# Sixteen instead of twenty-four projection groups, and eight heads of probabilities in flight, in a fused attention and expert layer

## The chip, the cores and the metric

One core of a Trainium2 chip runs the whole kernel in one launch. The core has TensorE (PE, matrix products), VectorE (DVE), ScalarE (ACT), GpSimd (POOL) and SyncE (SP, here used only to issue DMAs), each with its own instruction stream; they meet only at semaphores. SBUF is the memory of 128 partitions that all of them share, PSUM the eight banks that PE writes to. The metric is the device time of one execution in microseconds; lower is better.

## What is computed

One transformer layer on x of shape [32, 256, 128], all in float32:

```
xn = layernorm(x)
Q, K, V = xn @ W_qkv            # 16 heads of 64, per sample of 256 tokens
Q, K[first 32 of 64] = q * cos + rotate_half(q) * sin
scores = where(causal, -inf, Q K^T) / sqrt(64);  attn = softmax(scores) V
out = x + attn @ W_o + moe(xn)
moe: softmax over 9 logits, the top 2 chosen; 8 experts of 128 -> 512 (gelu) -> 128,
     the ninth choice passes xn through; each weighted with its gate
```

`rotate_half` takes the halves (x1, x2) of a head's 32 rotary values to (-x2, x1).

## The kernel before

**Stages.** A prologue loads and normalises all 64 tiles of tokens and transposes them (`xnT_hi`, `xnT_lo`: each float32 is split in two float16 numbers, and a product of two such pairs is three float16 matmuls, `split3`). Then the projections of sample 0 are made, the router decides (DVE), and the attention loop runs over 32 samples. Last come the experts over 104 tiles of sorted tokens and the gathering of their results.

**A sample** is 16 steps, one head each. On every engine a step `s` of sample `b` does the work of several heads, each a fixed number of steps behind:

- PE: scores of head s (4 matmuls, `scores`), then the projection units that `BESIDE[s]` lists (for the next sample, or the output product `y` of the last one), then the three transposes of head s-3's probabilities (`T_LAG`), and in every second step the product with V for two heads (`attend`, `PV_LAG` 5).
- DVE: `invert` (reciprocal of head s-2's sums), `mask` (causal mask and row maximum), an eviction of transposes for every fourth head, the work on a unit's result one step later (`turn`, `rest_low`, `y_add`), low parts of k's rotated rows (`k_rope_low`), low part of the attention output (`o_low`); in step 0 `dispatch` (normalises two tiles of tokens to `send_x` after waiting that the four sends of the sample before have landed) and `mix`.
- ACT: `rest_high`, `o_high`, transposes' evictions, `rope_high`, and the two exponentials of head s (`exps`).
- POOL: `scale` of head s-2 (two instructions, L432 and L433), `q_rope_low` (L422), `rope_add` (L417), and in steps 1, 9, 12 and 14 (`SEND_AT`) one indirect DMA (`send`, L437) that scatters 128 token rows to DRAM. Before each of the last three sends, and so before the scale of that step, POOL waits for the send before it (L448).
- SP: `stack_q(b + 1)` once q's rotated low parts are done, then `stack_k(b + 1)`.

**Projection units.** Q and K weights lie in 24 groups of 128 rows: 8 of rotary rows (four heads x 32 rows each), 8 of the other rows, and 8 more with the rotary rows in swapped order, so that `rotate_half` comes out of the matmul. A `rope` unit (8 a sample) makes one group and its swapped twin side by side in a PSUM bank; DVE multiplies the 512 columns with a table of cos and sin (`turned`, two buffers), POOL adds the two halves to `roped` (four buffers), ACT rounds to float16, POOL (q) or DVE (k) makes the low part. A `rest` unit (4 a sample) makes two groups without rotation. Three PSUM banks (`PJ`) go round among the units; two hold scores, two transposes, one the products with V.

**Stacking.** The scores product contracts over 128 partitions: 64 values of a head twice. SP's DMAs gather them inside SBUF: for each r of 4, two DMAs of 64 rows x 4 KB for q and two of 64 rows x 2 KB for k, 16 DMAs and 3 MB a sample. PE waits in steps 0, 4, 8 and 12 for group r = s/4 of both. The stacks have two buffers, the staging tiles (`q_staged`, `k_staged`) one.

The order on each engine is the order written in the code; nothing is reordered by a planner.

## Time and profile before

| | |
|---|---|
| median of 3 runs | 1582.79 us (1578.91 to 1585.89) |
| span of the profiled execution | 1643.9 us |
| looped samples 1 to 30 | 146.72 to 1190.99 us of the span |
| busy share PE, ACT, DVE, POOL | 82%, 71%, 70%, 60% |
| DMA share in the loop | about 0.44 |

The span goes from the first to the last instruction of one execution under the profiler; that execution has no other time, and it is 61 us longer than the median of the others. The first `L1108` of a sample is its first scores matmul: the tile it reads changes between `second` and `arena` from sample to sample, which is how a sample's start is found. A line number is a line of the kernel before.

### The profile page before, as it was taken

To read this page: it belongs to the slowest core of one execution; us is meant where nothing else is said; L and a number is where in the kernel's file an instruction comes from. 1 tells how busy PE (TensorE), PEld (TensorE's weight loads), DVE (VectorE), ACT (ScalarE), POOL (GpSimd) and SP (SyncE) were. 2 spreads that over 40 slices of the span, in tenths; PEclk is the share of its full clock that TensorE was granted. 3 is DMA by queue.
4 is the path that set the end of the run, shared out by engine and by line. 5 is a ranking of instruction groups with operands and counts; after the bars stand their busy time and mean duration, and the time that the engine had idled before them with its cause. 6 is when DMAs were issued, how large, how long until landed. Compare 5 with 4: busy or idle time off the path is not lost.

```text
span 1643.9 us, 48543 instructions
## 1 busy us (share of the span) xinstructions
PE 1341.7 (82%) x13156; PEld 1038.9 (63%) x13157; DVE 1143.8 (70%) x4325; ACT 1174.3 (71%) x3758; POOL 987.4 (60%) x1697
## 2 busy tenths in 40 slices
PE   2529999999999999999999999999977999576620
PEld 1417766777666776766777667766656988455520
DVE  6788776777777777767777777777756777354531
ACT  7409887888888888878888878888877888334310
POOL 3208777777777787777777777776760000454555
PEclk9859999999999999999999999999998999788865
DMA  9623544334553335543345433355423333222242
GB/s 302 164 49 83 115 115 102 86 84 97 115 119 87 86 84 109 120 104 86 85 93 117 117 91 85 84 110 117 105 89 94 87 85 85 72 77 77 79 129 64
DMA packets 125894, 166.49 MB, mean 101 GB/s; under 512 B 15504, under 2 KB 85392, under 8 KB 125456
## 3 DMA queue, kind: packets, MB, share of 16 engines
q1 hardware_dynamic: 117296, 147.50, 37.6%
q0 software_dynamic: 8416, 17.33, 3.6%
q14 instruction: 161, 1.32, 0.3%
q8 instruction: 21, 0.34, 0.1%
HBM read 30.42 MB, written 33.69 MB: 39 GB/s over the span
## 4 chain that ended last, share of the span: by engine, by line
POOL 30%; issue 20%; PE 18%; DMA 16%; DVE 7%; another core or an unknown queue 3%; ACT 2%; DVEq 1%; POOLq 1%; SPq 1%; ACTq 0%
DMA sorted_x_dram<-send_x,send_at 15%; POOL probs L433 8%; POOL probs L432 7%; POOL arena L417 7%; PE bank L1034 4%; PE bank L1033 4%; PE bank L1035 4%; POOL arena L422 4%; POOL sorted_x_dram L437 3%; PE bank L1132 1%; PE bank L1166 1%; PE bank L1118 1%; DVE arena L690 1%; POOL arena L482 1%
## 5 line engine op out<-in xcount | busy, mean ns | idle before, releaser
L577 ACT ACTIVATE probs<-arena,neg_max 128x128 f32<-128x128 f32 (+1 forms) x1024 | 455.4, 448 | 126.5 <-DVE neg_max L887 112.1
L432 POOL TENSOR_TENSOR probs<-probs,inv_total 128x128 f32<-128x128 f32 x512 | 208.2, 407 | 247.8 <-DMA sorted_x_dram<-send_x,send_at 126.4
L1118 PE MATMUL bank<-ident,probs 128*128 128x128 f32 x1536 | 263.2, 280 | 70.6 <-POOL probs L433 62.6
L887 DVE CUSTOM_DVE_ANT_0 arena<-bank,causal 128x128 f32<-128x128 f32 (+1 forms) x1024 | 314.9, 345 | 0.0
L482 POOL DMA_INDIRECT arena<-sorted_y_dram,slots x128 | 123.7, 967 | 273.6 <-DMA sorted_y_dram<-arena 171.6
L1118 PEld LDWEIGHTS bank<-ident,probs 128*128 128x128 f32 x1536 | 173.6, 141 | 144.9 <-issue 87.9
L894 DVE RECIPROCAL inv_total<-total 128x2 f32<-128x2 f32 x512 | 82.9, 162 | 254.4 <-PE bank L1109 178.1
L433 POOL TENSOR_SCALAR probs<-probs,inv_total 128x256 f32<-128x256 f32 x512 | 251.4, 491 | 0.0
L417 POOL TENSOR_TENSOR arena<-arena 128x256 f32<-128x256 f32 x256 | 189.8, 752 | 64.0 <-DVE arena L849 58.8
L1033 PE MATMUL bank<-xnT_lo,wqk_hi 128*128 (+1 forms) x768 | 212.2, 276 | 10.7 <-DVE arena L855 10.2
L1035 PE MATMUL bank<-xnT_hi,wqk_hi 128*128 (+1 forms) x768 | 212.1, 276 | 0.0
L1034 PE MATMUL bank<-xnT_hi,wqk_lo 128*128 (+1 forms) x768 | 211.9, 276 | 0.0
L577 ACT ACTIVATION_READ_ACCUMULATOR probs<-arena,neg_max 128x1 f32 x1024 | 195.3, 191 | 0.0
L558 ACT ACTIVATE probsT<-bank 128x384 f32<-128x384 f32 x384 | 186.0, 484 | 9.4 <-issue 9.0
L1132 PE MATMUL bank<-probsT,second 128*64 128x256 f32 x1024 | 169.2, 406 | 1.0 <-DVE arena L905 1.0
L849 DVE TENSOR_TENSOR arena<-bank,arena 128x512 f32<-128x512 f32 x256 | 169.2, 681 | 1.1 <-PE bank L1035 0.9
L437 POOL DMA_INDIRECT sorted_x_dram<-send_x,send_at x128 | 140.0, 1094 | 29.0 <-issue 21.0
L533 ACT ACTIVATE arena<-arena 128x256 f16<-128x256 f32 x256 | 106.7, 417 | 59.8 <-POOL arena L417 53.1
L1033 PE MATMUL bank<-second,arena 128*128 x640 | 123.4, 225 | 12.4 <-issue 8.5
L1034 PE MATMUL bank<-second,arena 128*128 x640 | 122.4, 225 | 13.4 <-issue 13.4
L636 ACT ACTIVATE arena<-bank 128x512 f32<-128x512 f32 x160 | 92.9, 598 | 55.4 <-remote 30.9
L1035 PE MATMUL bank<-second,arena 128*128 x640 | 121.8, 224 | 11.8 <-issue 11.6
(158 smaller groups left out, 3675.6 us busy)
## 6 DMA issues: line engine op xcount, KB each, us to landing
second<-arena SPq DMA_DIRECT2D x128, 256.0 KB, 4.2
arena<-arena SPq DMA_DIRECT2D x128, 256.0 KB, 4.1
second<-arena SPq DMA_DIRECT2D x128, 128.0 KB
arena<-arena SPq DMA_DIRECT2D x128, 128.0 KB
arena<-sorted_x_dram SPq DMA_DIRECT2D x80, 128.0 KB
sorted_y_dram<-arena SPq DMA_DIRECT2D x80, 128.0 KB
sorted_x_dram<-arena SPq DMA_DIRECT2D x3, 2560.0 KB, 21.2
arena<-experts_dram SPq DMA_DIRECT2D x8, 512.0 KB, 4.5
```

What stands on the lines that cost most here:

```text
L417: nc.gpsimd.tensor_tensor(roped[j % 4], t[:, 0:SEQ], t[:, SEQ:2 * SEQ], ALU.add).then_inc(rope_sum, 1)
L432: nc.gpsimd.tensor_tensor(p0, p0, inv_total[:, s % 4, 0:1].broadcast_to([P, P]), ALU.mult)
L433: nc.gpsimd.tensor_scalar(p1, p1, inv_total[:, s % 4, 1:2], 1.0, ALU.mult, ALU.mult).then_inc(p_ready, 1)
L437: nc.gpsimd.indirect_dma_start(out=sorted_x, out_offset=bass.IndirectOffsetOnAxis(ap=send_at[:, i:i + 1], axis=0), in_=send_x[:, i // TOP, ...
L558: nc.scalar.activation(probsT[:, s % 4, :], TP[s % 2][:, 0:PW], ACT.Copy).then_inc(t_out[1], 1)
L577: last = nc.scalar.activation(probs[:, s % 4, at:at + w], masked[:, s % 2, at:at + w], ACT.Exp, bias=neg_max[:, s % 2, t:t + 1], scale=-1. ...
L887: last = nc.vector.tensor_tensor_reduce(out=masked[:, s % 2, at:at + w], in0=SC[s % 2][:, at:at + w], in1=causal[:, at:at + w], scale=1.0, ...
L1033: mm(dst, a_hi, b_lo, start=start, stop=False)
L1034: mm(dst, a_lo, b_hi, start=False, stop=False)
L1035: return mm(dst, a_hi, b_hi, start=False, stop=stop)
L1118: last = nc.tensor.transpose(TP[s % 2][:, k * P:(k + 1) * P], probs[:, s % 4, k * P:(k + 1) * P], ident[:])
L1132: mm(PV[rows, :], v_sb[:, 0, vs], probsT[:, s % 4, 0:SEQ], start=True, stop=False)
```

## The change

The swapped copies of the rotary rows go away (24 groups become 16). The rotary rows are regrouped instead: a group now holds the first 16 rotary rows of eight heads, its partner the last 16 of the same heads. A `rope` unit makes such a pair, [x1 | x2] in one bank; DVE multiplies both by cos and both by sin (two instructions of 512 columns), POOL makes x1 cos - x2 sin and x2 cos + x1 sin (two instructions of 256). There are 4 rope units a sample instead of 8, one unit a step, and low and high parts are made on 512 columns at once. `by_cos` and `by_sin` have one buffer, `roped` two. The staging tiles hold rotary halves in another row order, so each r takes five DMAs instead of two for q and five for k (one of 64 rows, four of 32 rows whose sources are 16 rows): 40 a sample.

The freed PSUM bank (PJ goes from 3 to 2) gives a second bank for the products with V. The buffers of probabilities and their sums go from 4 to 8 heads; transposes run 4 steps behind instead of 3, evictions 5 instead of 4, products with V 7 instead of 5, the output 8 instead of 6. The identity tile and `half` move into the arena. The weights' high and low parts are made in 16 instructions each instead of one.

```diff
-PROLOGUE = ([("rest", 0), ("rest", 1)] + [("rope", j) for j in range(4)]
-            + [("rest", 2), ("rest", 3)] + [("rope", j) for j in range(4, 8)] + [("v_low", 0), ("v_low", 1)])
+PROLOGUE = [("rest", 0), ("rest", 1), ("rope", 0), ("rope", 1), ("rest", 2), ("rest", 3), ("rope", 2), ("rope", 3),
+            ("v_low", 0), ("v_low", 1)]
 BESIDE = [
-    [("rest", 0)], [("rest", 1), ("rope", 0)], [("rope", 1)], [("rope", 2), ("rope", 3)],
-    [("rest", 2)], [("rest", 3), ("rope", 4)], [], [("rope", 5), ("rope", 6)],
-    [("rope", 7)], [("v_high", 0), ("v_high", 1)], [], [("y", 0)],
-    [("v_low", 0)], [("y", 1)], [("v_low", 1)], [],
+    [("rest", 0)], [("rope", 0)], [("rest", 1)], [("rope", 1)],
+    [("rest", 2)], [("rope", 2)], [("rest", 3)], [("rope", 3)],
+    [("v_high", 0)], [], [("v_high", 1)], [("y", 0)],
+    [("y", 1)], [("v_low", 0)], [("v_low", 1)], [],
 ]
 SEND_AT = [1, 9, 12, 14]
-PJ_BANKS = 3
+PJ_BANKS = 2
+ROPES = 4
+POS = (0, 2, 1, 3)
+STACKED = 16 * 5
-INV_LAG, T_LAG, OUT_LAG, PV_LAG, O_LAG = 2, 3, 4, 5, 6
+INV_LAG, T_LAG, OUT_LAG, PV_LAG, O_LAG = 2, 4, 5, 7, 8
+HELD = 8
...
-        PJ, SC, TP = bank[0:3], bank[3:5], bank[5:7]
-        PV = bank[7][:, 0:SEQ]
+        PJ, SC, TP = bank[0:2], bank[2:4], bank[4:6]
+        PV = [b[:, 0:SEQ] for b in bank[6:8]]
...
-                sp.wait_ge(q_rope_lo, 4 * n + 4)
+                sp.wait_ge(q_rope_lo, 2 * n + 2)
                 for r in range(GRP):
-                    for half_at in range(2):
-                        sp.dma_start(q_stack[parity][64 * half_at:64 * half_at + 64, r, :, :].rearrange("p l n -> p (l n)"),
-                                     q_staged[32 * r:32 * r + 32, :, :, :].rearrange("p k l n -> p (k l n)")).then_inc(q_stacked[r], 16)
+                    sp.dma_start(q_stack[parity][64:128, r, :, :, :].rearrange("p h l n -> p (h l n)"),
+                                 q_rest[32 * r:32 * r + 32, :, :, :].rearrange("p h l n -> p (h l n)").unsqueeze(1)
+                                 .broadcast_to([32, 2, 2048])).then_inc(q_stacked[r], 16)
+                    for h in range(2):
+                        for c in range(2):
+                            rows = slice(64 * h + 16 * r, 64 * h + 16 * r + 16)
+                            sp.dma_start(q_stack[parity][32 * c:32 * c + 32, r, h, :, :].rearrange("p l n -> p (l n)"),
+                                         q_rope[rows, c, :, :].rearrange("p l n -> p (l n)").unsqueeze(1)
+                                         .broadcast_to([16, 2, 1024])).then_inc(q_stacked[r], 16)
...
-                sp.wait_ge(k_rope_lo, 4 * n + 4)
+                sp.wait_ge(k_rope_lo, 2 * n + 2)
                 for r in range(GRP):
-                    for half_at in range(2):
-                        sp.dma_start(k_stack[parity][64 * half_at:64 * half_at + 64, NG * r:NG * r + NG, :].rearrange("p h t -> p (h t)"),
-                                     k_staged[32 * r:32 * r + 32, half_at, :, :]).then_inc(k_stacked[r], 16)
+                    sp.dma_start(k_stack[parity][64:128, r, :, :].rearrange("p h n -> p (h n)"),
+                                 k_rest[32 * r:32 * r + 32, :, :, :].rearrange("p l h n -> p l (h n)")).then_inc(k_stacked[r], 16)
+                    for h in range(2):
+                        for c in range(2):
+                            rows = slice(64 * h + 16 * r, 64 * h + 16 * r + 16)
+                            sp.dma_start(k_stack[parity][32 * c:32 * c + 32, r, h, :],
+                                         k_rope[rows, c, :, :]).then_inc(k_stacked[r], 16)
...
-                nc.gpsimd.tensor_tensor(roped[j % 4], t[:, 0:SEQ], t[:, SEQ:2 * SEQ], ALU.add).then_inc(rope_sum, 1)
+                r = roped[j % 2]
+                nc.gpsimd.tensor_tensor(r[:, 0, :], by_cos[:, 0, :], by_sin[:, 1, :], ALU.subtract)
+                nc.gpsimd.tensor_tensor(r[:, 1, :], by_cos[:, 1, :], by_sin[:, 0, :], ALU.add).then_inc(rope_sum, 1)
...
-                    raw(wqk_hi[:].rearrange("p g n -> p (g n)"), raw_qk)
+                    for at, of in WQK:
+                        last = nc.scalar.activation(wqk_hi[:, at, :], of, ACT.Copy, scale=W_SCALE)
+                    last.then_inc(raw_hi, 1)
...
                 dve.wait_ge(pj_ready, u + 1)
-                if not (isinstance(m, int) and m == 0 and j < 2):
-                    dve.wait_ge(rope_sum, 8 * m + j - 1)
-                nc.vector.tensor_tensor(turned[j % 2], psum[:], rot_q if j < NG else rot_k,
-                                        ALU.mult).then_inc(turn_done, 1)
+                if not (isinstance(m, int) and m == 0 and j == 0):
+                    dve.wait_ge(rope_sum, ROPES * m + j)
+                nc.vector.tensor_tensor(by_cos, both, cos, ALU.mult)
+                nc.vector.tensor_tensor(by_sin, both, sin, ALU.mult).then_inc(turn_done, 1)
```

## Rows read from the trace of the kernel before

**Rows 1.** The page: span, and busy time, share and instructions of each engine.

```profile
span 1643.9 us, 48543 instructions
...
PE 1341.7 (82%) x13156; PEld 1038.9 (63%) x13157; DVE 1143.8 (70%) x4325; ACT 1174.3 (71%) x3758; POOL 987.4 (60%) x1697
```

**Rows 2.** Busy time by stretch, one sample in the middle; last columns clock, DMA, GB/s.

```profile
146.72:180.60 33.88, 32.10 (x309) 24.55 (x310) 26.42 (x118) 29.68 (x103) 25.62 (x48) 1.00 0.51 114
...
390.23:425.13 34.90, 32.45 (x311) 24.43 (x309) 26.48 (x116) 29.31 (x103) 26.66 (x49) 1.00 0.44 99
425.13:1190.99 765.86, 714.02 (x6776) 537.34 (x6777) 578.22 (x2528) 638.26 (x2199) 579.17 (x1057) 1.00 0.44 99
```

**Rows 3.** Waits in that sample: engine, line, releaser; us, times, longest.

```profile
POOL probs L432 <- DMA sorted_x_dram<-send_x,send_at: 4.3, 2, 2.9
...
PE bank L1118 <- POOL probs L433: 1.7, 4, 0.6
...
POOL arena L417 <- DVE arena L849: 1.4, 2, 0.7
...
PE bank L1118 <- ACT probsT L558: 0.5, 1, 0.5
```

**Rows 4.** Timeline of POOL in that sample.

```profile
397.73 0.73 POOL L417 TENSOR_TENSOR arena<-arena 128x256 f32<-128x256 f32 x1 [0.69 <-DVE arena L849]
...
413.08 1.18 POOL L437 DMA_INDIRECT sorted_x_dram<-send_x,send_at  x1 [0.16 <-issue]
...
419.07 0.40 POOL L432 TENSOR_TENSOR probs<-probs,inv_total 128x128 f32<-128x128 f32 x1 [2.94 <-DMA sorted_x_dram<-send_x,send_at]
...
423.43 0.40 POOL L432 TENSOR_TENSOR probs<-probs,inv_total 128x128 f32<-128x128 f32 x1 [1.41 <-DMA sorted_x_dram<-send_x,send_at]
```

**Rows 5.** Groups in that sample: busy us, mean ns; idle before, releaser.

```profile
L432 POOL TENSOR_TENSOR probs<-probs,inv_total 128x128 f32<-128x128 f32 x16 | 6.5, 404 | 6.0 <-DMA sorted_x_dram<-send_x,send_at 4.3 <-DVE inv_total L894 1.4
...
L417 POOL TENSOR_TENSOR arena<-arena 128x256 f32<-128x256 f32 x8 | 5.9, 753 | 1.6 <-DVE arena L849 1.4
...
L437 POOL DMA_INDIRECT sorted_x_dram<-send_x,send_at x5 | 5.4, 1080 | 0.8 <-issue 0.8
L849 DVE TENSOR_TENSOR arena<-bank,arena 128x512 f32<-128x512 f32 x8 | 5.3, 682 | 0.0
...
L422 POOL TENSOR_TENSOR arena<-arena 128x256 f16<-128x256 f32 x4 | 2.7, 682 | 0.0
```

**Rows 6.** Timeline of PE at the start of that sample: start, duration.

```profile
390.56 0.27 PE L1033 MATMUL bank<-xnT_lo,wqk_hi 128*128 x1
...
391.10 0.27 PE L1035 MATMUL bank<-xnT_hi,wqk_hi 128*128 x1
391.95 0.32 PE L1118 MATMUL bank<-ident,probs 128*128 128x128 f32 x1 [0.58 <-POOL probs L433]
```

**Rows 7.** Timeline of DVE in that sample, step 0.

```profile
392.49 0.60 DVE L828 TENSOR_SCALAR send_x<-acc,neg_mean,rstd 128x128 f32 x2 [0.46 <-DMA sorted_x_dram<-send_x,send_at]
```

**Rows 8.** Timeline of SP's DMA issues in that sample.

```profile
406.79 8.03 SPq L311 DMA_DIRECT2D arena<-arena  x8
415.82 6.45 SPq L318 DMA_DIRECT2D arena<-arena  x8
```

**Rows 9.** Chain that ended last, before the first looped sample.

```profile
132.20 0.54 SPq L311
...
142.10 4.39 DMA arena<-arena
...
146.72 0.23 PE bank L1108
```

**Rows 10.** Issues of three DMA lines: ns min/median/max, first and last start.

```profile
L311 SPq DMA_DIRECT2D arena<-arena x128: 537/1057/2015, 132.2 to 1180.5; - x128
...
L318 SPq DMA_DIRECT2D arena<-arena x128: 597/603/1697, 141.3 to 1188.2; - x128
...
L302 SPq DMA_DIRECT2D arena<-experts_dram x8: 327/429/435, 1191.4 to 1234.7; - x8
```

More of the change, by code:

```diff
@@ L255, in beside, with rest_parts, rope_parts @@
                     for n, (at, kind, j) in enumerate(units_of(first, last)) if at == s]
-        def parts(which, rest, g, n=1):
-            at = slice(g * SEQ, (g + n) * SEQ)
-            if which == 0:
-                return q_staged[:, rest, 0, at], q_staged[:, rest, 1, at]
-            return k_staged[:, 0, rest, at], k_staged[:, 1, rest, at]
+        def rest_parts(j):
+            return [q_rest[:, j % 2, n, :] if j < 2 else k_rest[:, n, j % 2, :] for n in range(2)]
+        def rope_parts(j):
+            of, at = q_rope if j < 2 else k_rope, slice(j % 2 * SEQ, (j % 2 + 1) * SEQ)
+            return [of[:, :, n, at] for n in range(2)]
         def owner(kind, b):
@@ L451, in sample @@
                     for kind, j, u, psum, n in beside(b, first, last, s - 3):
-                        if kind == "rope" and j < NG:
+                        if kind == "rope" and j < 2:
                             q_rope_low(j, b + 1)
@@ L700, in _ @@
                     low(rw_lo[:], rw_f[:], rw_hi[:], 1).then_inc(split, 1)
-                    low(wqk_lo[:].rearrange("p g n -> p (g n)"), raw_qk,
-                        wqk_hi[:].rearrange("p g n -> p (g n)"), 2).then_inc(split, 1)
+                    for at, of in WQK:
+                        hi, lo = wqk_hi[:, at, :], wqk_lo[:, at, :]
+                        if at < 8:
+                            hi, lo = (v.rearrange("p (r n) -> p r n", n=16) for v in (hi, lo))
+                        last = low(lo, of, hi, 2)
+                    last.then_inc(split, 1)
             low(wvo_lo[:].rearrange("p k n -> p (k n)"), raw_vo, wvo_hi[:].rearrange("p k n -> p (k n)"), 3).then_inc(split, 1)
@@ L1124, in attend @@
                     pe.wait_ge(v_ready, 4 * b + (2 if j == 0 else 4))
-                if not (first and j < 1):
-                    pe.wait_ge(o_done, 8 * b + j)
+                if not (first and j < 2):
+                    pe.wait_ge(o_done, 8 * b + j - 1)
                 for i in range(2):
@@ L1141, in sample @@
                     if not (first and s < T_LAG):
-                        transposes(G - T_LAG, (s - T_LAG) % 4, None if first and s < T_LAG + 2 else
+                        transposes(G - T_LAG, (s - T_LAG) % HELD, None if first and s < T_LAG + 2 else
                                    evicted(b, s - T_LAG - 2) if s >= T_LAG + 2 else evicted(b - 1, s - T_LAG - 2 + H))
```

153 lines of the change are left out of this document (82 added, 71 removed).

## The prediction

> **What bounds the kernel now.** I read the page first [rows 1]: no engine is full over the span (PE 82%, ACT 71%, DVE 70%, POOL 60%), so I cut it at the sample starts. The 30 looped samples run from 146.72 to 1190.99, 1044.3 us or 34.81 us each, at full TensorE clock [rows 2]. That stretch is 64% of the span and the change works almost only there; what lies before (147 us, mostly router and normalising) and behind (453 us, the last sample and the experts) keeps its work.
>
> Inside one typical sample (390.23 to 425.13) PE is busy 32.45 of 34.90 us, ACT 29.3, DVE 26.5, POOL 26.7 [rows 2]. PE looks like the limit, but its list of waits names POOL: before the transposes it waits 1.7 us for L433 and 0.5 for an ACT eviction that is itself one step behind [rows 3]. POOL in turn stands 4.3 us, twice, on the landing of an indirect send: the send issued at 413.08 is waited for until 419.07, 2.9 us of it with nothing else to do [rows 3, 4]. So POOL with 26.7 busy + 4.3 landing waits + 0.8 before the sends [rows 5] = 31.8 us is a chain that PE hangs on with a lag of only three heads; the other 3.1 us of its sample are waits for DVE (1.4 + 1.4, [rows 3, 5]) and crumbs. It is a two-way coupling: a late POOL delays PE, a late PE then starves POOL at the start of the next sample.
>
> **The change, part by part.**
>
> *Four projection units fewer on PE.* A rope unit is six matmuls; the six at 390.56 to 391.10 start 0.11 us apart [rows 6], so a unit is 6 x 0.109 = 0.655 us and four are 2.6 us a sample. PE's own need falls from at most 32.45 to at most 29.8 us (busy time counts overlapping tails, so the true need is lower). ACT's need stays under the 29.3 it has now.
>
> *The same rotation elsewhere.* DVE multiplied 8 x 512 elements (0.68 us each, [rows 5]); it now makes two 512-element multiplications for each of four units: 8 again. POOL added 8 x 256 (0.75 us) and still does. The four low parts of 256 (0.68 us) become two of 512, on POOL and on DVE: between half of now (only fixed cost) and all of it; I take the same. So DVE 26.5 and POOL 26.7 us are not relieved. The two products have one buffer now instead of two, so a turn waits for POOL's add of the unit before; units are two steps apart, which covers it (an add pair is 1.5 us against about 4 us of steps).
>
> *The longer pipeline (transposes four heads behind instead of three, values seven instead of five, eight probability buffers, two PV banks).* It hides POOL's landing stalls from PE: 1.7 + 0.5 us and the shadow they throw. It does not remove them from POOL: sends stay at steps 1, 9, 12 and 14. POOL's 31.8 us therefore remain as a cycle: add of unit 0, the scales, sends 1 to 3, landing of send 3, dispatch on DVE at step 0 (L828 already waits for it, [rows 7]), turn of unit 0, add of unit 0. The bound is 31.8 if sends land as now, and 29.3 if both landing waits shrink to what the slower steps cover (31.8 - 2.5: I leave 1.8 of 4.3). PSUM for projections goes from three banks to two, with one unit a step; the bank is read in the step after, so this costs nothing while DVE is less than a step late, and makes PE follow DVE's local pace when it is.
>
> *The stacking DMAs.* Now 8 for q and 8 for k a sample; afterwards 20 and 20 for the same 3 MB. Here I see the new danger. Today SP issues q over 8.03 us from 406.79, then k over 6.45 us from 415.82 [rows 8]. The first heads of the next sample need only k's group 0, but that is queued behind all of q. At the first looped boundary this chain already decides: q's first issue at 132.20, k's group 0 landed, PE starts at 146.72 [rows 9]: 14.5 us from rotation done to start. In the loop it has room: 406.79 + 14.5 = 421.3 against 425.13, 3.8 us.
>
> After the change the chain has 25 issues instead of 10. What does one cost? No row shows a copy of 32 rows inside SBUF. Floor: 0.33 us, the shortest issue of L302; ceiling: 0.64 us, the unblocked 0.60 of a 64-row k copy (L318) and 0.04 between issues [rows 8, 10]. Above L318's floor, q's median of 1.06 us is the 256 KB waiting for the queue. The form is nearest to L318's (three-dimensional source, SBUF on both sides), but half the rows; I take 0.58 spacing. Then q is 4 x 1.0 + 16 x 0.58 = 13.3 us at most, 11.6 if the large ones no longer queue; I take 12.3; k's first five 2.9 us; last landing about 1.6 us more: 16.8 us. Both ends: the bytes alone, as now, 14.0 less what overlaps, say 13.2 (spacing 0.37); 4 x 1.1 + 16 x 0.64 + 5 x 0.64 + 2.3 = 20.1.
>
> Where does it start? Now rotation of q is done 16.6 us after the sample's start (406.79 - 390.23) [rows 8]. The work up to there is the same on POOL (five scales, four adds of 256, low parts), but the first add can start earlier: it stands at 7.5 us (397.73, [rows 4]), of which about 1 us is PE's stall of 0.58 before the first transposes and its echo [rows 6]. So 15.5 us, minus little. The next sample can start at 15.5 + 16.8 = 32.3 us; ends 28.7 and 35.6.
>
> *A rule against the change.* A 64-row k copy of 128 KB goes out every 0.64 us, 205 GB/s, its source 32 partitions wide [rows 8, 10]. If the 16-partition sources drained at half that rate, the rope half of q (1 MB) would take 10.2 us instead of 5.1, q in all 15.3, and k's group 0 1.9 more with about 1 us landing: 18.2, so a sample of 33.7. The Trainium skill, page SBUF — State Buffer, section on the DMA port swizzle, says just this: a range of 16 partitions reaches 4 ports and one of 32 reaches 8, 104 against 189 GB/s at 1 MiB; its figure for the wide case fits the 205 seen here, and no run here shows the narrow one. By the page the estimate would be near that same 33.7 a sample.
>
> *Weights and prologue.* 16 weight groups instead of 24 but split by 16 instructions on ACT and DVE: before, 3,072 columns in one; now 2,048 in sixteen. About even. Ten units instead of fourteen before the router, where DVE's own work decides: nothing, give or take 2 us. The first boundary, already set by stacking, gets 16.8 - 14.5 = 2.3 us longer. Two more lags to drain at the end: +1 us, against a shorter stall.
>
> **The sum.** Two cycles lie almost on each other: POOL with its sends 31.8, stacking 32.3. I take 32.1 us a sample: 30 x (34.81 - 32.1) = 81 saved, less 2.3 and 1 = about 78 us of the profiled 1643.9 (there is no other time for that execution; it is 61 us above the median 1582.8, so it carries profiling cost). Taken off the median: 1505 us.
>
> **The rivals.**
> - *A, both cycles near 32 (31.2 to 33.2 a sample)*: 1477 to 1538. For it: two independent sums meet. 0.45.
> - *B, stacking stays hidden and the sends land earlier*, because small copies spread the traffic; the bound is then PE's 29.8 or POOL's 29.3, samples of 29.3 to 31.2: 30 x 3.6 to 5.5 less the 3.3 at the edges, so 1421 to 1477. For it: the 0.33 us issue. Against: DVE's dispatch still waits for send 3. 0.25.
> - *C, narrow sources at half rate*, or 0.64 and a queue: 33.2 to 34.5 a sample, 1538 to 1577. 0.15.
> - *D, no change*: the stall only moves from before the transposes to the sample's first scores, 34.5 to 35.0, 1577 to 1592. 0.05.
> - *E, slower*: SP's queue decides. With the start at 15.5 us the point is 34.8 - 15.5 = 19.3 us for 25 issues and a 1.6 us landing: 0.71 us a copy. At 0.80 us it is 21.6 us, a sample of 37.1, 30 x 2.3 = 69 us more and the 3: 1655. Against: no unblocked issue in the trace is over 0.6. 0.10.
>
> Range: out of it stay D and E (0.15) and the lowest fifth of B (0.05): 1432 to 1578. A's own range is 1477 to 1538. Faster by over 0.5% (8 us, about what a measurement of this kernel tells from no change): A, B, C = 0.85; within: 0.05; slower: 0.10.
>
> **What would show it.** Right: sample starts 32 us apart; PE's waits before L1118 for POOL gone in the loop; a wait of one to three us before the first L1108 of a sample, released by a stacking DMA; POOL still waiting some 3 to 4 us a sample for sends; PE busy about 30 of 32; L311's successor issued in about 12 us. Wrong: no DMA in front of L1108 (then B); spacing of narrow copies over 0.7 us (E); packets of 2 KB from 16 partitions lasting twice those of now (C); PE waiting for its projection banks on DVE, which I cost at nothing: if that shows, DVE's first nine steps of a sample are the limit, and a sample is longer by what it waits there. The step I trust least is the cost of a copy with 32 rows.

## The result

The changed kernel is slower: 1649.26 us (median of 4, 1642.40 to 1653.47) against 1580.85 us of the kernel before, a ratio of 1.041 [1.037, 1.045]. The forecast was 1505 us, its range 1432 to 1578. The outcome is that of rival E (1655 us, chance 0.10), and a part of the reason is E's.

From the page after, the span, the engines' busy time and SP's DMA queue:

```profile
span 1640.7 us, 46858 instructions
...
PE 1285.1 (78%) x12388; PEld 977.4 (60%) x12389; DVE 1115.2 (68%) x4276; ACT 1143.0 (70%) x3645; POOL 981.5 (60%) x1635
...
q1 hardware_dynamic: 145968, 147.03, 40.8%
```

Two spans can't be compared here. That of [rows 1] is 1643.9 and this one 1640.7, though the medians lie 68 us apart: behind the last head's scores (1221.3 before, 1278.6 after, from the trace) the execution of before took 422.6 us and this one 362.1. That is the expert stage, which both kernels share; it is told of at the end. So I compare samples, by the start of the first scores matmul of each.

Busy time by stretch: the 30 looped samples, then two samples in a row, then the step 0 of each of the two.

```profile
155.93:1251.98 1096.05, 939.39 (x8520) 683.86 (x8521) 761.47 (x3390) 835.05 (x2880) 783.13 (x1380) 0.95 0.46 95
376.58:413.04 36.46, 31.37 (x284) 22.84 (x285) 25.40 (x113) 27.75 (x97) 26.10 (x46) 0.95 0.46 95
413.04:448.00 34.96, 29.80 (x284) 21.94 (x285) 25.40 (x113) 27.73 (x97) 26.10 (x46) 1.00 0.48 99
376.58:380.27 3.69, 3.69 (x21) 2.40 (x22) 2.01 (x10) 1.34 (x6) 0.85 (x2) 0.57 0.45 101
413.04:415.26 2.22, 2.21 (x21) 1.68 (x21) 1.59 (x9) 0.85 (x4) 0.86 (x2) 1.00 0.35 83
```

A looped sample takes 1096.05 / 30 = 36.54 us, against 34.81 [rows 2]: 52 us of the 68. PE did lose its four units (29.80 us busy at full clock, against 32.45 [rows 2]; the forecast was at most 29.8), and every engine is less busy than before. What has grown is waiting, and PE's largest wait is in one place. Waits of the loop:

```profile
POOL probs L461 <- DVE inv_total L932: 229.3, 131, 6.3
...
PE bank L1145 <- DMA arena<-arena: 44.7, 15, 4.9
...
PE bank L1145 <- DMA second<-arena: 40.5, 15, 3.7
...
PE bank L1072 <- DVE arena L895: 34.2, 72, 1.5
...
POOL probs L461 <- DMA sorted_x_dram<-send_x,send_at: 26.0, 38, 2.4
```

L1145 is the scores matmul (L1108 before): in each of the 30 samples PE waits for a stacking DMA before its first head, 85.2 us in all, 2.8 us each. POOL's 4.3 us a sample for its sends [rows 3] have shrunk to 26.0 / 30 = 0.9, and POOL now waits 7.6 us a sample for DVE, which waits for PE: POOL is no longer a limit. L1072 <- L895 is the two-bank wait that I priced at nothing: 1.1 us a sample.

SP's issues of the first of those samples, and then the end of the chain to the next sample's start:

```profile
393.25 0.56 SPq L323 DMA_DIRECT2D second<-arena  x1
393.86 2.90 SPq L329 DMA_DIRECT2D second<-arena  x4
396.81 0.59 SPq L323 DMA_DIRECT2D second<-arena  x1
397.44 3.21 SPq L329 DMA_DIRECT2D second<-arena  x4
400.70 0.60 SPq L323 DMA_DIRECT2D second<-arena  x1
401.34 2.96 SPq L329 DMA_DIRECT2D second<-arena  x4
404.35 0.59 SPq L323 DMA_DIRECT2D second<-arena  x1
404.99 3.10 SPq L329 DMA_DIRECT2D second<-arena  x4
408.13 0.59 SPq L336 DMA_DIRECT2D second<-arena  x1
408.76 2.51 SPq L341 DMA_DIRECT2D second<-arena  x4
```

```profile
392.10 1.13 POOL arena L449
...
394.50 0.99 SPq L329
...
398.08 1.30 SPq L329
...
410.68 2.13 DMA second<-arena
412.82 0.23 issue
413.05 0.23 PE bank L1145
```

The first issue comes 16.7 us after the sample's start, q's 20 copies take 14.9 us, k's first five 3.1, and 1.8 later PE starts: 19.8 us of chain, and 36.5 in all. It replaces q's and k's rows of [rows 8]. The issue times, by line (L329 and L341 are the new 32-row copies, 16 source rows; ns min/median/max):

```profile
L329 SPq DMA_DIRECT2D second<-arena x256: 591/597/1845, 75.1 to 1209.6; - x128
```

```profile
L341 SPq DMA_DIRECT2D arena<-arena x256: 591/596/783, 151.8 to 1259.5; - x128
```

A copy of 32 rows costs SP what one of 64 rows did [rows 10]: 0.60 us, and 0.04 to the next. In each of the four q groups one 32-row copy takes longer, 1.0 to 1.3 us (two stand in the chain above).

There is a second loss that I hadn't thought of. After PE's wait its clock is at half: the 21 matmuls of step 0 take 3.69 us at a granted clock of 0.57 in the one sample and 2.22 us at 1.00 in the other. The other engines' step 0 follows, and q's first issue with it: 16.7 us after the start there, 15.1 us here (428.15 - 413.04).

All 30 samples fit this: from q's first issue to the next sample's start it is 19.5 to 20.3 us in each but the first two (20.9 and 21.3), and the samples differ by when that issue comes, 15.1 us after the start in the five even ones at full clock, 16.1 in the one odd sample at full clock, and 16.4 to 17.4 in the 24 whose step 0 ran below it. So each of them is the time to q's first issue plus a chain that hardly varies. The mean clock of the loop is 0.95 where it was 1.00 [rows 2], so about 110 us of it ran at 1.2 GHz. The Trainium skill, page TensorE: Matmul & The Clock Gate, section HAM oscillation, describes this pattern, a burst of matmuls, a wait for a DMA, and the next burst at half clock; the trace agrees in 24 of 30 samples, with 2.8 us of wait a sample on average and 1.5 us more for step 0 in the sample shown. The length of the wait alone doesn't tell the 24 from the other six: those waited 2.4 to 2.6 us, and one of the 24 waited 2.3.

### The profile page after: what moved, and what is told of

Its sections match the earlier page's. It is cut to its first block, busy times and chain, and to the rows that moved or that the text cites. A ratio compares the mean times of both kernels' runs of the same rounds, so it can differ in the third digit from the quotient of the medians.

```text
span 1640.7 us, 46858 instructions
## 1 busy us (share of the span) xinstructions
PE 1285.1 (78%) x12388; PEld 977.4 (60%) x12389; DVE 1115.2 (68%) x4276; ACT 1143.0 (70%) x3645; POOL 981.5 (60%) x1635
## 3 DMA queue, kind: packets, MB, share of 16 engines
q1 hardware_dynamic: 145968, 147.03, 40.8%
## 4 chain that ended last, share of the span: by engine, by line
PE 25%; SPq 24%; POOL 19%; issue 12%; DVE 10%; DMA 7%; ACT 2%; DVEq 1%; POOLq 0%; ACTq 0%
SPq L329 17%; PE bank L1072 5%; PE bank L1073 5%; PE bank L1074 4%; POOL arena L511 4%; SPq L323 4%; POOL probs L462 3%; PE bank L1170 3%; POOL probs L461 3%; POOL arena L449 3%; SPq L341 3%; PE bank L1156 2%; POOL arena L444 2%; DMA arena<-sorted_y_dram,slots 2%; DMA second<-arena 2%
## 5 line engine op out<-in xcount | busy, mean ns | idle before, releaser
L1156 PE MATMUL bank<-arena,probs 128*128 128x128 f32 x1536 | 265.2, 283 | 33.7 <-ACT probsT L589 26.6
L1156 PEld LDWEIGHTS bank<-arena,probs 128*128 128x128 f32 x1536 | 188.5, 146 | 82.9 <-ACT probsT L589 31.1
L1072 PE MATMUL bank<-xnT_lo,wqk_hi 128*128 (+1 forms) x512 | 150.8, 294 | 41.5 <-DVE arena L895 35.0
L943 DVE TENSOR_TENSOR arena<-bank,arena 128x256 f16<-128x256 f32 x256 | 106.6, 416 | 88.2 <-ACT arena L594 88.2
L466 POOL DMA_INDIRECT sorted_x_dram<-send_x,send_at x128 | 145.5, 1136 | 29.6 <-issue 20.3
L1074 PE MATMUL bank<-xnT_hi,wqk_hi 128*128 (+1 forms) x512 | 149.4, 292 | 0.0
L1145 PE MATMUL bank<-second 128*128 128x128 f16 (+1 forms) x512 | 103.8, 256 | 52.3 <-DMA second<-arena 40.5
L443 POOL TENSOR_TENSOR arena<-arena 128x256 f32<-128x256 f32 x128 | 105.5, 824 | 61.7 <-DVE arena L890 61.7
L1145 PE MATMUL bank<-arena 128*128 128x128 f16 (+1 forms) x512 | 104.0, 257 | 47.1 <-DMA arena<-arena 44.7
L564 ACT ACTIVATE arena<-arena 128x512 f16<-128x512 f32 x128 | 80.7, 630 | 71.8 <-POOL arena L444 71.7
L1072 PE MATMUL bank<-second,arena 128*128 x640 | 118.5, 222 | 3.1 <-DVE arena L1020 2.9
L1020 DVE TENSOR_TENSOR arena<-arena 128x512 f16<-128x512 f32 x160 | 109.4, 693 | 14.5 <-ACT arena L674 11.5
```

The costliest lines, as they stand in the source:

```text
L1072: mm(dst, a_hi, b_lo, start=start, stop=False)
L1074: return mm(dst, a_hi, b_hi, start=False, stop=stop)
L1145: mm(dst, q_lo, ks, start=True, stop=False)
L1156: last = nc.tensor.transpose(TP[s % 2][:, k * P:(k + 1) * P], probs[:, at, k * P:(k + 1) * P], ident[:])
```

## The experiments

Where only a ratio tells, it is against the kernel before in the same batch; its median there was 1584 us for e1, e3, e5 and e6, 1655 for e9 to e12, 1583 for e13 to e15, 1656 for e16 and 1653 for e17 to e19. Periods are means of the 30 looped samples, "odd" those that begin a turn of the loop (two samples a turn, so samples 1, 3, ...).

| run | ratio | interval | us a sample | odd / even |
|---|---|---|---|---|
| before | 1 | | 34.81 | 34.7 / 34.9 |
| after | 1.041 | 1.037 to 1.045 | 36.54 | 36.7 / 36.4 |
| e1 half the bytes | 1.038 | 1.035 to 1.040 | 36.76 | 36.8 / 36.7 |
| e6 before, 40 copies | 1.040 | 1.037 to 1.042 | 36.85 | 37.1 / 36.6 |
| e5 after, old lags | 1.030 | 1.027 to 1.033 | 36.30 | 36.2 / 36.5 |
| e3 k's group 0 earlier | 1.019 | 1.016 to 1.022 | 35.81 | 38.1 / 33.6 |
| e9 unrotated rows first | 1.004 | 1.003 to 1.006 | 35.20 | 37.1 / 33.3 |
| e10 the same, 32 copies | 1.002 | 1.001 to 1.003 | 34.90 | 36.6 / 33.2 |
| e11 as e9, old lags | 1.001 | 1.000 to 1.003 | 34.96 | 37.3 / 32.6 |
| e12 before, two banks | 1.148 | 1.145 to 1.150 | 42.77 | 42.9 / 42.7 |
| e13 as e10, 6 samples a turn | 0.978 | 0.976 to 0.979 | 33.55 | |
| e14 before, 6 a turn | 1.010 | 1.008 to 1.012 | 35.23 | |
| e15 after, 6 a turn | 1.057 | 1.054 to 1.060 | 37.64 | |
| e16 as e10, no jump | 0.962 | 0.961 to 0.964 | 32.75 | |
| e17 after, PE kept busy | 1.022 | 1.019 to 1.024 | 35.91 | 36.8 / 35.0 |
| e18 before, no jump | 0.992 | 0.989 to 0.995 | 34.45 | |
| e19 as e9, no jump | 0.963 | 0.961 to 0.966 | 32.78 | |

**Bytes or issues?** e1 moves half the bytes of each 32-row copy in the looped samples (q's low parts and half of k's columns are not copied there, so the scores are made of old data):

```diff
+                                sp.dma_start(q_stack[parity][32 * c:32 * c + 32, r, h, 0, :],
+                                             q_rope[rows, c, 0, :].unsqueeze(1).broadcast_to([16, 2, 512])).then_inc(q_stacked[r], 16)
...
+                            w = slice(0, 512) if isinstance(n, int) else slice(0, 256)
+                            sp.dma_start(k_stack[parity][32 * c:32 * c + 32, r, h, w],
+                                         k_rope[rows, c, :, w]).then_inc(k_stacked[r], 16)
```

> The changed kernel, with the 32 narrow stacking copies of a looped sample (16-row sources) moving half their bytes: the low parts of q's rotated rows and half of the columns of k's are not copied again after the first two samples, so the scores use stale values there. The number of copies and of everything else stays. Theory M (SP's issue queue: about 0.64 us a copy whatever it carries; the sample's period is the time to q's rotation, 16.7 us, plus 20 q copies, 5 k copies and a landing, 19.6 us): nothing moves, samples 36 to 37 us, 1640 to 1655 us. Rival R1 (16-partition sources drain at half rate): q's narrow megabyte would take about 5 us less, samples of 32 to 33 us, under 1560 us. Rival R2 (two projection banks make PE follow DVE): no change, as in M. Rival R3 (the longer lags): no change.

36.76 us a sample, nothing gained. Neither the bytes nor a rate of the narrow sources sets the chain, so C's first condition is out (its other one, 0.64 us a copy and a queue, is near the mechanism that was found, at too low a price). The profile pages say a little more on the narrow sources. SP's queue before:

```profile
q1 hardware_dynamic: 117296, 147.50, 37.6%
```

After, the packets of nearly the same bytes took 40.8% of nearly the same span, 8 per cent more. About 50 of the 147 MB now come from 16-row sources (1.5 MB in each of 32 samples); half the rate for those would have been about a third more, by my estimate. What their rate would be without the issues as the limit no run here shows.

**Are the copies alone enough?** e6 is the kernel before, its 16 copies cut into 40 for the same bytes.

```diff
-                    for half_at in range(2):
-                        sp.dma_start(q_stack[parity][64 * half_at:64 * half_at + 64, r, :, :].rearrange("p l n -> p (l n)"),
-                                     q_staged[32 * r:32 * r + 32, :, :, :].rearrange("p k l n -> p (k l n)")).then_inc(q_stacked[r], 16)
+                    sp.dma_start(q_stack[parity][0:64, r, :, :].rearrange("p l n -> p (l n)"),
+                                 q_staged[32 * r:32 * r + 32, :, :, :].rearrange("p k l n -> p (k l n)")).then_inc(q_stacked[r], 16)
+                    for i in range(2):
+                        for l in range(2):
+                            sp.dma_start(q_stack[parity][64 + 32 * i:96 + 32 * i, r, l, :],
+                                         q_staged[32 * r + 16 * i:32 * r + 16 * i + 16, :, l, :]).then_inc(q_stacked[r], 16)
```

> The kernel before, with its 16 stacking copies of a sample cut into 40 that carry the same 3 MB to the same places (for each r one copy of 64 rows and four of 32 rows from 16-row sources, for q and for k); nothing else of the change. M: 10 copies ahead of the next sample's first scores become 25, the chain grows from 14.4 to about 19.6 us behind a start at 16.6 us, samples of 36 to 37 us instead of 34.8, and the clock falls at the wait: 1620 to 1655 us. R2 and R3: neither is in this kernel, so it stays at 1575 to 1590 us. R1: half of the bytes come from narrow sources, slower too, as in M.

1.040, the whole loss without any other part of the change (the diff shows q; k's copies are cut likewise). Its stretch and its waits:

```profile
153.19:1258.55 1105.36, 995.63 (x9241) 758.12 (x9242) 788.60 (x3450) 868.39 (x3000) 788.54 (x1440) 0.96 0.47 94
```

```profile
POOL probs L439 <- DMA sorted_x_dram<-send_x,send_at: 95.0, 53, 3.4
...
PE bank L1115 <- DMA second<-arena: 43.2, 15, 4.0
...
PE bank L1115 <- DMA arena<-arena: 27.2, 14, 4.3
```

The same wait at the first scores (L1115) and the same clock below 1.00, with the old projections, lags and banks. So 36.8 us is what 40 copies in this order cost here with PE's work as it was, and 36.5 with four units fewer.

**What is the pipeline worth?** e5 is the changed kernel with the lags of before.

```diff
-INV_LAG, T_LAG, OUT_LAG, PV_LAG, O_LAG = 2, 4, 5, 7, 8
+INV_LAG, T_LAG, OUT_LAG, PV_LAG, O_LAG = 2, 3, 4, 5, 6
```

> The changed kernel with the lags of before (transposes 3, evictions 4, values 5, output 6 heads behind); rotary regrouping, ring of eight and two banks for the values stay. M: the stacking chain sets the sample anyway, 36 to 37.5 us, 1635 to 1670 us; if a late POOL now also delays q's rotation, the upper end. R3 (the longer lags cost the time): back to 1575 to 1600 us or below. R2: no change.

1 per cent faster than the changed kernel: 0.2 us a sample, 7 us in the loop, the rest at its edges and behind. Under this chain the longer pipeline brings nothing.

**The order of the copies.** e3 puts k's group 0 behind q's groups 0 and 1 in place of behind all of q. e9 also sends the unrotated rows' eight copies ahead of everything, as soon as their low parts are there, with semaphores of their own, so that their staging tiles are free sooner; e10 merges the rotated rows' copies so that 32 are left; e11 is e9 with the old lags.

The diff is e9's; `rest_copies`, `q_group` and `k_group` hold the copies of before under new names (4 unrotated of q or of k, 4 of one r of q, 4 of one r of k).

```diff
+                rest_copies(n, parity, 0)
                 sp.wait_ge(q_rope_lo, 2 * n + 2)
-                for r in range(GRP):
...
+                for r in (0, 1):
+                    q_group(parity, r)
+                rest_copies(n, parity, 1)
...
                 sp.wait_ge(k_rope_lo, 2 * n + 2)
-                for r in range(GRP):
...
+                k_group(parity, 0)
+                for r in (2, 3):
+                    q_group(parity, r)
+                for r in (1, 2, 3):
+                    k_group(parity, r)
```

> The changed kernel with the 40 stacking copies in another order: q groups 0 and 1, then k group 0, then q 2 and 3, then k 1 to 3. Same copies, same computation. M: k's group 0 leaves after 10 copies instead of 20, at 23 us of the sample instead of 31.5 (if k's rotation is done by then), the wait before the first scores goes, with it the clock's fall; the next bound is POOL with its sends, 31 to 33.5 us a sample, 1490 to 1560 us. R2: the banks still hold PE, samples stay at 35 us or more, 1590 us or more. R1: the copies still drain slowly, but fewer stand ahead: faster as well, so this run does not tell it from M.

> The changed kernel with the same 40 stacking copies, issued earlier and freed earlier: the four copies of q's unrotated rows go as soon as those are made, those of k's likewise after q's rotated groups 0 and 1; then k group 0, q 2 and 3, k 1 to 3. The unrotated rows count on semaphores of their own, so that their staging tile is free as soon as they have left. Same computation. Theory M (the queue of copies, in front of the first scores and in front of the reuse of the staging tiles, sets the sample): 12 copies between q's rotation and k's group 0 instead of 25, about 8 us less; neither wait binds, samples of 31 to 32.5 us by the next bound (POOL with its sends, DVE with the two banks), 1475 to 1520 us. Rival R2 (two banks and DVE's pace hold the sample by themselves at 35 us or more): 1590 us or more. Rival R4 (the 40 copies slow the sends and everything else by being there): over 34 us a sample, over 1560 us.

> The run with the unrotated rows first, with k's narrow copies merged in pairs (one of 64 rows per r and half instead of two of 32; the order of the contraction's rows is changed for q and k alike): 32 copies a sample. Same computation. M: if the queue no longer binds with 40 copies, eight fewer bring at most 1 us a sample: the same as the run with 40, or up to 2% less. If the queue still binds there: a clear gain, 2 us a sample or more, 60 us.

> The run with the unrotated rows first, with the lags of before (3, 4, 5, 6 heads). M with the stacking hidden: now PE hangs on POOL's sends again, and the longer lags show what they are worth: samples 1 to 3 us longer than in the run with the long lags, 30 to 80 us more. Rival R3 (the longer lags cost, as the 1% that they lost under the stacking chain suggests): the same or faster than that run.

In all four the wait at the first scores is gone, and three of them miss what M (the theory that SP's queue sets the sample) expected all the same: e3 took 1615 us where 1490 to 1560 were expected, e9 came out at 1.004 of the kernel before where 1475 to 1520 us (0.93 to 0.96) were expected, and e11 isn't 1 to 3 us a sample longer than e9 but 0.2 shorter. (e10 against e9 is as expected, no more than 2 per cent less.) The gain stops short for a reason that only the single samples show: on average the even ones take 32.6 to 33.6 us, the odd ones 36.6 to 38.1. Sample 1, which is odd but has no jump of the loop in front of it, takes 32.2 to 32.7 us in e9, e10 and e11. Two neighbours of e10, odd and even:

```profile
216.36:253.11 36.75, 31.44 (x285) 22.63 (x285) 25.29 (x113) 27.66 (x96) 26.18 (x46) 0.95 0.49 94
253.11:286.34 33.23, 30.02 (x287) 21.89 (x285) 25.20 (x113) 27.85 (x99) 26.07 (x46) 1.00 0.56 105
```

DVE at the start of the odd one, then of the even one:

```profile
217.16 0.42 DVE L961 TENSOR_TENSOR arena<-bank,arena 128x256 f16<-128x256 f32 x1 [1.62 <-ACT arena L612]
220.39 0.17 DVE L950 RECIPROCAL inv_total<-total 128x2 f32<-128x2 f32 x1 [2.81 <-issue]
...
254.29 0.42 DVE L961 TENSOR_TENSOR arena<-bank,arena 128x256 f16<-128x256 f32 x1 [1.62 <-ACT arena L612]
254.63 0.15 DVE L950 RECIPROCAL inv_total<-total 128x2 f32<-128x2 f32 x1
```

Between the same two instructions DVE stands still for 2.81 us, put down to issue, and there lies the branch back to the top of the loop. From the end of each branch to the first record of the next turn the trace has 2.8 us on DVE and 2.7 on ACT, 0.2 on POOL and 0.1 on PE (medians of 14 turns; in the kernel before 2.8, 2.6, 0.2 and 0.1). DVE is then behind, PE waits in step 2 for the projection bank that L913 reads (2.5 us), and its clock falls, to 0.95 over the sample. So the two banks do cost something here; whether a third would cover the jump wasn't run.

e11 against e9 says again that the longer lags bring nothing: with them even samples are 0.7 us longer, odd ones 0.2 shorter.

**Two banks.** e12 is the kernel before with two banks for projections.

```diff
-PJ_BANKS = 3
+PJ_BANKS = 2
...
-        PJ, SC, TP = bank[0:3], bank[3:5], bank[5:7]
+        PJ, SC, TP = bank[0:2], bank[3:5], bank[5:7]
```

> The kernel before with two projection banks instead of three; the third lies idle. M: it has two units in steps 1, 3, 5, 7 and 9, so PE waits for DVE's reading there; that costs up to 1 us a sample, 1580 to 1615 us. R2 (the bank is what costs the changed kernel its 4%): 1620 us or more.

A miss by far: 8.0 us a sample. PE waits for DVE's reading of a bank, in the turn of a rope unit (L849) and in the low part of a rest unit (L855). Over the loop, 156.1 to 1439.3:

```profile
PE bank L1033 <- DVE arena L849: 156.7, 119, 1.9
PE bank L1033 <- DVE arena L855: 95.0, 82, 3.0
```

Together that is 8.4 us a sample, against 0.2 with three banks (6.2 us in the loop before, all for L855). This kernel has two units in some steps; the changed kernel, with one a step, waits 1.1 us for the same. That the second unit in a step makes the difference is argued, not shown by a run.

**Is it the jump?** e13 is e10 with six samples in a turn of the loop, e14 and e15 the kernels before and after with six, e16 is e10 with the 30 samples written out.

```diff
-            with eng.Fori(0, B // 2 - 1) as i:
-                body(2 * i + 1, 1, False, False)
-                body(2 * i + 2, 0, False, False)
+            with eng.Fori(0, (B - 2) // SAMPLES) as i:
+                for m in range(1, SAMPLES + 1):
+                    body(SAMPLES * i + m, m % 2, False, False)
```

> The kernel with the unrotated rows copied first and 32 copies a sample, whose looped samples alternate between 33.2 us and 36.7 us, with six samples in one turn of the loop instead of two (30 samples, 5 turns instead of 15). Theory 'jump': the long samples are long since VectorE and ScalarE stand still for 2.0 to 2.9 us behind the jump back to the loop's top, which every second sample begins with; then 10 of the 15 long samples become short ones, 10 x 3.5 = 35 us, a mean period of 33.8 us and a ratio to the kernel before of 0.980 to 0.985. Theory 'odd samples': they are long for what the two halves of the stacks or the samples' parity do, whatever the loop's turns; then the alternation stays and the ratio stays at 1.002.

> The kernel before with six samples in one turn of the loop. Its own engines stand still behind the jump too (2.1 us on VectorE, 2.0 us on ScalarE), but its samples do not alternate: 34.8 us each. Theory 'the jump is covered in the kernel before, by the slack that its third projection bank leaves': within 5 us of no change. Theory 'the jump costs in every kernel': 10 x 2 us or more less, a ratio of 0.985.

> The changed kernel with six samples in one turn of the loop. Its first scores of a sample wait some 2.8 us for k's copies, and the jump of VectorE lies inside that wait. Theory 'the copies' chain sets the period': within 5 us of the changed kernel, ratio 1.035 to 1.042. Theory 'the jump sets it here too': 25 to 35 us less, ratio near 1.02.

e13 gives 1548.3 us against 1583.4. Its samples with no jump before or behind them take 32.9 us, odd or even: parity is out, and the stall goes with the jump. But the jump itself has grown, which my theory had not: with six samples a turn PE and POOL stand still too. The sample in front of a jump, one without, and PE at the jump:

```profile
315.54:352.41 36.87, 30.04 (x286) 21.83 (x285) 25.65 (x114) 30.43 (x106) 26.18 (x47) 1.00 0.55 104
282.66:315.54 32.88, 29.87 (x286) 21.89 (x285) 25.23 (x113) 27.51 (x97) 26.56 (x47) 1.00 0.59 109
```

```profile
348.06 0.55 PE L1178 MATMUL bank<-arena,probs 128*128 128x128 f32 x3 [0.76 <-ACT probsT L608]
352.41 0.23 PE L1167 MATMUL bank<-arena 128*128 128x128 f16 x1 [3.81 <-issue]
```

3.8 us, where PE showed nothing with two samples a turn (some 570 matmuls instead of 1,710). That is why e14 is slower than before, where I expected no change: the four samples in front of a jump take 38.2 us, about 4 more than the others, those behind one 35.5, and away from the jumps it is 34.6 us, little less than 34.8. e15 is slower by more than its four jumps: 37.64 us a sample, and the 26 samples not in front of a jump take 36.7 to 39.3, 37.5 on average. That is a miss of both its theories. Its trace shows step 0 at 3.2 to 4.2 us in every sample, where six samples of the changed kernel had it at 2.2; why it never escapes the half clock I don't know.

The trace holds one hint of what the engines stand still for. Its DMA queues named instruction moved 8 packets in the 5.5 us around the jump shown (348.5 to 354), one in as long a stretch in front of it (320 to 325.5), and one around a sample's start in e16 (345 to 350.5). That would fit code being loaded anew at a jump; no run shows it as the cause.

> The kernel with the unrotated rows copied first and 32 copies a sample, its 30 looped samples written out one after the other, without a jump. With six samples a turn it took 32.9 us a sample, and at each of the 4 jumps TensorE stood still for 4.0 us with the clock at half speed behind it (36.9 us for the sample before the jump, 33.6 to 34.5 us for the one behind it). Theory 'the jump is what costs': 32.9 us for each of the 30, 4 x 5 = 20 us less than with six, about 1528 us, a ratio of 0.965 to the kernel before. Rival 'the stall comes from the amount of code, wherever it is read': with 30 samples of code in a row the engines stand still between samples too, and the time is the same as with six or more.

Here both the jump and its stall are gone: 30 samples of 32.73 to 33.0 us, the clock at 1.00 throughout, 1593.0 us against 1656.0, ratio 0.962. Its loop, then SP's issues of one sample that starts at 381.34 (the next starts at 414.08, the rotated q rows go out from 397.18):

```profile
151.91:1134.34 982.43, 893.86 (x8523) 655.46 (x8521) 757.71 (x3390) 824.38 (x2881) 780.46 (x1381) 1.00 0.57 106
```

```profile
390.39 3.56 SPq L322 DMA_DIRECT2D arena<-arena  x4
397.18 6.30 SPq L333 DMA_DIRECT2D arena<-arena  x8
403.52 2.53 SPq L326 DMA_DIRECT2D arena<-arena  x4
406.10 1.25 SPq L339 DMA_DIRECT2D arena<-arena  x2
```

k's group 0 is issued by 407.4, 6.7 us before it is needed.

**Chain or clock, and whose gain?** e17 leaves the changed kernel's copies alone and gives PE 20 multiplications (2.2 us) whose result nobody reads ahead of the wait, into a bank of scores that is overwritten next; the wait for that bank moves ahead of them. e18 is the kernel before written out, e19 is e9 (40 copies) written out.

```diff
+                if s == 0 and not first:
+                    for _ in range(20):
+                        mm(SC[0][:, 0:2 * P], wqk_hi[:, 0, :], xnT_hi[:, 0:2 * P], start=True, stop=True)
                 if s % GRP == 0:
                     pe.wait_ge(q_stacked[s // GRP], STACKED * b + STACKED)
```

> The changed kernel, and ahead of the wait for k's copies TensorE multiplies 20 times 256 columns (some 20 x 0.11 = 2.2 us at full clock, less than the 2.7 us that it stands still there) into the bank of scores that it is about to overwrite; nothing reads them. The copies are left as they are. Theory 'two parts, the longer chain and the clock': with TensorE busy the half clock behind the wait goes, step 0 falls from 3.4 us to 2.2 us, VectorE finishes q's rows 1.4 to 1.8 us earlier and the period becomes that of the six samples that ran at full clock, 35.0 us: 30 x 1.5 = 45 us less than the changed kernel, a ratio to the kernel before of 1.010 to 1.018. Rival 'the clock is a by-product': the period stays at 36.5 us and the ratio at 1.04.

> The kernel before with its 30 looped samples written out one after the other. Its samples that touched no jump took 34.5 us in the kernel with six samples a turn, against 34.8 us with two: 10 us less, a ratio of 0.993. If a jump cost it as much as it cost the kernel with the unrotated rows first (3.5 us in every second sample), 50 us less, 0.968.

> All 40 copies of the changed kernel, the unrotated rows' 8 first, its samples written out one after the other. Theory 'the order of the copies is what matters, not their count': the rotated rows' 32 copies take 32 x 0.64 = 20.5 us and q's 16 of them 10.2 us + k's first four and their landing 4.7 us = 14.9 us behind the end of q's rotation at 15.5 us, which is 30.4 us and less than the 32.8 us of the other engines: the same 32.8 us a sample as with 32 copies, a ratio of 0.962 to 0.967. Rival 'SyncE's queue still sets the period': 34 us or more a sample, over 0.98.

An even and an odd sample of e17:

```profile
408.43:443.47 35.04, 32.13 (x304) 23.82 (x305) 25.40 (x113) 27.59 (x96) 26.08 (x46) 1.00 0.48 99
443.47:480.01 36.54, 31.97 (x305) 23.94 (x306) 25.32 (x113) 27.67 (x97) 26.09 (x46) 1.00 0.46 94
```

More work on PE makes the changed kernel faster, by 0.63 us a sample, 19 us in the loop. Even samples take 35.0 us, as expected; odd ones keep 36.8 on average (36.7 before). Step 0 takes 2.2 us in 29 of the 30 samples, but the odd ones that begin behind a jump now show a stall of PE of 1.0 to 2.5 us some 5 to 7 us after their start, which the even ones don't have, and q's first issue comes 15.5 to 18.4 us after the start in place of 15.1; in four of them the clock falls behind that stall, to 0.96 over the sample. In the changed kernel the slow step 0 hides most of it: behind a slow step 0 no sample there has such a stall of over 1.0 us. So I had the clock's part right and had left out what was beneath it, and the ratio is 1.022, not 1.010 to 1.018.

e18 at 0.992 is what was expected, and e19 at 0.963 too: 40 copies cost no more than 32 once k's group 0 isn't behind them all. Between e18 and e16 lie 3 per cent, 34.45 against 32.75 us a sample: what the rest of the change is worth once the copies are in another order and both kernels are free of the jump (taken from two batches, and the kernel before wasn't run with its copies in that order). The version to keep is e16 or e19, 63 and 58 us below the kernel before in their batches.

## Why the prediction was wrong

**The step that failed** is the term "16.8 us" of the stacking chain: "q is 4 x 1.0 + 16 x 0.58 = 13.3 us at most, ... I take 12.3", k's five 2.9, the landing 1.6. Measured in the sample shown: 14.9, 3.1 and 1.8, 19.8 us. It lies near the far end that I had worked out and left (20.1). The row nearest to the new copies, L318's 0.60 [rows 10], was right to 0.01 us; I took 0.58 for half the rows although nothing showed that rows matter, and I let the 1.0 us of the large copies shrink because the small ones would give the queue air, whereas the delay moved on to a small copy in each group of q. With 0.64 for 21 copies and 1.1 for one in each of q's groups, as at my far end, and the landing of 1.8, the chain is 19.6 us and the sum 15.5 + 19.6 = 35.1 us a sample: no gain at all. Six samples that ran at full clock measure 34.6 to 36.0, and e17's even ones 35.0.

**The two terms that were missing** turn no gain into a loss. Half clock behind the wait: where it is away, even samples of the changed kernel take 35.0 us, with it samples take 36.3 to 37.9. And the jump of the loop, which e17 laid bare (36.8 us in odd samples). Of the 1.73 us lost a sample, 0.2 is then the chain alone (35.0 against 34.81) and 1.5 the clock and the jump, of which the clock's removal by itself gives back 0.6. The changed kernel written out without the jump wasn't run, so how the rest divides is open. I had named a wait of one to three us before the first scores as a sign of being right; I didn't ask what a wait of nearly 3 us does to the clock.

**By the other steps.** *Four units fewer on PE*: right, 29.8 us. *The start at 15.5 us*: right at full clock (15.1), 16.7 behind a half-clock step. *POOL's cycle of 31.8 us*: not seen as a limit. Its landing waits fell to 0.9 us a sample, where I had expected them to stay at 3 to 4, and e16 shows 32.7 us with POOL waiting 3.2 us a sample for DVE's `inv_total`. Whether POOL would hold the kernel if the sends were slower wasn't tried. That e16's 32.7 us lie near the 32.1 of the sum confirms neither of its two cycles: k's group 0 has 6.7 us to spare there, and what sets those 32.7 I didn't work out. *The longer pipeline*: worth nothing here (e5, e11), in place of the 2.2 us of stalls I gave it to hide. *Two banks at nothing*: nearly right in the changed kernel (1.1 us, and e17's even samples, which wait 0.7 for it, issue q's first copy at the same 15.1 us), but not behind a jump (2.5 us in e9 and e10) and not to be carried over (e12: 8.0 us). *Prologue and first boundary*: the first scores start 4.8 us later (107.5 against 102.7), sample 0 is 4.4 us longer; I had 2.3 for the two together. *Where the profiled execution's 61 us come from*: not from profiling, as I wrote, but from the expert stage.

**By the rivals.** E's condition came true on average: 18.0 us for 25 issues is 0.72 a copy, its point was 0.71, and the 19.8 us chain is just over its 19.3, although most copies take no more than the 0.64 that spoke against it. That alone gives no more than 35 us a sample. E's 1655 us had asked for 0.80 a copy; that the time came so near it is luck, since clock and jump did the rest, and no rival had them. D (the stall only moves) is the nearest description of the changed kernel at full clock. A and B had the same false term. The upper bound of the range, 1578 us, left out just what the far end of the chain gives (35.6 us a sample, about 1610 us by the same sum).

The Trainium skill, page DMA: Bandwidth & Descriptors, section Issuing engines are not separate DMA queues, says that the time to start a DMA "is usually small relative to the DMA itself". For one copy that holds here: 0.64 us to issue, medians of 2.0 to 3.5 us from issue to landing. But landings overlap and issues don't: 40 issues at 0.64 take 25.6 us of SP's queue in a sample of 36.5, in which the DMA engines are busy 0.46 of the time, 16.8 us, and e1 halved what the small copies carry for no gain.

## What to carry to other kernels

Cost a chain of DMAs by issues, each at the full price of the nearest row whatever it carries, and put first in the queue what is needed first: 24 copies more cost 4 per cent with it last (e6), and with it first 40 copies took the same time as 32 (e19 and e16). When a wait moves to TensorE, add what the clock costs behind it. When the means of a loop disappoint, list its passes one by one: here every second one held a stall of 3 us that the means hid.

## What was not expected of the hardware

- *A jump's price*: 2.8 us on DVE and 2.6 on ACT with two samples a turn; with six (e13) 3.0 and 3.1, and besides 3.4 on POOL and 3.8 on PE. Written out, the same code ran without a stall between samples. What decides whether PE pays (the length of the code is what differed) was not settled.
- *An issue's price*: 0.60 us for an SBUF-to-SBUF copy on SP's queue, the same for 32 and 64 rows and from 16 KB (e1, k's small copies) to 256 KB (L323 of the changed kernel has a median of 0.60). One small copy in each group of q takes 1.0 to 1.3 us, the 256 KB copies of the kernel before have a median of 1.06 [rows 10]; that a full queue makes them wait would fit and isn't shown.
- *Two lengths of the same expert stage*: behind the last head's scores 357 to 363 us in the profiled executions of after, e1, e3, e5, e6 and e13 to e15, 423 to 432 in those of before, e9 to e12 and e16 to e19. Kernels that differ only ahead of it fall in both, and in the longer one there are gaps of 5 to 12 us on PE, ACT, DVE and POOL that the profile puts down to issue or remote. It goes with the batch, each of which ran on a chip of its own (the kernel before took 1583 and 1584 us there, 1653 to 1656 here; its profiled execution shown ahead of the prediction is of the longer kind, its median of the shorter). What makes it is open. It is why ratios within a batch and periods of samples are used above.
